# First attention: the value products of a batch in one visit, with sixteen probability buffers

## The reference

```
qkv = x @ Wqkv + bqkv                 # x: layer-normed rows of the batch
qkv_a = xa @ Wqkv_aux + bqkv_aux      # xa: the batch's 375 context rows
dots = einsum('bhqd,bhkd->bhqk', q, k) * scale       # 16 heads, 112 keys of the batch itself
dots_aux = einsum('bhqd,bhkd->bhqk', q, ka) * scale  # 375 keys of the context
h_main = softmax(dots) @ v
h_aux = softmax(dots_aux) @ va
out = h_main * (1 - sigmoid(g)) + h_aux * sigmoid(g)
return out @ Wo + bo
```

## Time and profile before

| what | value |
|---|---|
| median of three runs | 784.34 us (781.73 to 785.57) |
| span of the profiled execution | 792.0 us |
| PE busy | 724.7 us, 91% of the span, 6719 instructions |
| PE weight loads busy | 568.2 us, 6720 instructions |
| VectorE busy | 418.0 us, 53% |
| ScalarE busy | 326.5 us, 41% |
| a step of the first attention, from 301.50 | 23.38 us, PE busy 23.32 |

### The profile page before, as it was taken

How to read it: one execution, slowest core, us unless ns; L and a number is a source line. 1 busy time by engine, 2 the same in 40 slices (tenths; PEclk the granted TensorE clock), 3 DMA queues, 4 the chain that set the end, 5 groups by cost and what they waited for, 6 DMA issues and landing times. The chain is left out here.

```text
span 792.0 us, 19429 instructions
## 1 busy us (share of the span) xinstructions
PE 724.7 (91%) x6719; PEld 568.2 (72%) x6720; DVE 418.0 (53%) x1267; ACT 326.5 (41%) x884; POOL 219.5 (28%) x361
## 2 busy tenths in 40 slices
PE   4688999999999999998998699998999988999996
PEld 2445777666677766676665588888788778999995
DVE  2366777787777687774772322222488762111111
ACT  2215655566555566654544133331465551101110
POOL 2402332233332232330312013333355532111111
PEclk9869999999999999999999789999999998999999
DMA  4999977998888998885946549882566642999950
GB/s 154 130 137 118 165 113 120 126 123 134 145 140 146 150 144 118 147 141 81 121 129 191 141 120 246 247 220 63 170 197 205 195 131 60 306 337 335 334 174 16
DMA packets 98984, 128.12 MB, mean 162 GB/s; under 512 B 23363, under 2 KB 83884, under 8 KB 98769
## 3 DMA queue, kind: packets, MB, share of 16 engines
q1 hardware_dynamic: 90625, 115.24, 68.0%
q0 software_dynamic: 3824, 8.46, 4.1%
q10 hardware_dynamic: 4447, 3.30, 1.8%
HBM read 74.68 MB, written 23.88 MB: 124 GB/s over the span
## 5 line engine op out<-in xcount | busy, mean ns | idle before, releaser
L549 ACT ACTIVATE probs<-psum 128x448 f32<-128x448 f32 (+2 forms) x256 | 125.2, 541 | 60.5 <-PE psum L883 59.9
L755 DVE TENSOR_REDUCE neg_max<-psum 112x2 f32<-112x750 f32 x128 | 118.8, 928 | 8.9 <-PE psum L866 7.3
L866 PE MATMUL psum<-stacks 96*128 96x487 bf16 (+1 forms) x256 | 78.3, 389 | 8.6 <-DMA stacks<-q_parts 5.8
L883 PE MATMUL psum<-stacks 102*128 102x112 bf16 (+1 forms) x1024 | 77.5, 215 | 3.6 <-DMA stacks<-mt 2.0
L898 PEld LDWEIGHTS psum<-probs,rings 128*32 128x32 f32 (+2 forms) x2048 | 45.3, 109 | 46.9 <-issue 37.6
L883 PEld LDWEIGHTS psum<-stacks 102*128 102x128 bf16 (+1 forms) x1024 | 54.7, 99 | 33.0 <-ACT probs L549 23.9
L898 PE MATMUL psum<-probs,rings 128*32 128x112 f32 (+2 forms) x2048 | 76.7, 266 | 0.8 <-issue 0.8
L1947 PEld LDWEIGHTS psum<-e_xt,rings 128*128 128x128 f32 x512 | 59.5, 192 | 2.2 <-ACT e_xt L1893 1.3
L1947 PE MATMUL psum<-e_xt,rings 128*128 128x112 f32 x512 | 59.7, 275 | 0.9 <-ACT e_xt L1893 0.9
L1913 DVE SCALAR_TENSOR_TENSOR e_y<-psum,e_x_in 112x256 f32<-112x256 f32 x16 | 7.7, 484 | 98.0 <-PE psum L1961 98.0
L1961 PE MATMUL psum<-rings,e_hid 128*112 128x256 f32 x256 | 57.9, 379 | 1.3 <-DVE e_hid L1920 1.3
(11 more groups left out here) (226 smaller groups left out, 1389.2 us busy)
## 6 DMA issues: line engine op xcount, KB each, us to landing
rings<-in_L_ffn_w SPq DMA_DIRECT2D x32, 1024.0 KB, 7.1
stacks<-rings SPq DMA_DIRECT2D x96, 243.5 KB
ct_dram<-rings SPq DMA_DIRECT2D x16, 375.0 KB, 10.8
a_ct<-ct_dram SPq DMA_DIRECT2D x16, 375.0 KB, 5.1
a_ctx<-in_ctx SPq DMA_DIRECT2D x16, 375.0 KB
stacks<-q_parts SPq DMA_DIRECT2D x96, 56.0 KB
rings<-in_ctx SPq DMA_DIRECT2D x16, 256.0 KB
w<-in_L_ffn_W SPq DMA_DIRECT2D x8, 512.0 KB, 11.5
```

The costliest lines, as they stand in the source:

```text
L549: nc.scalar.activation(probs[k % 4][0:keys, :, :], src, ACT.Exp, scale=DH ** -0.5).then_inc(s["exp_done"], 1)
L755: nc.vector.tensor_reduce(neg_max[:, 0, h:h + 2], psum[0:T, pair:pair + 2, 0:S], AX, ALU.max, negate=True)
L866: last = nc.tensor.matmul(bank[2 - 2 * (k % 2) + j][0:rows, 0:KV], q_flat[n.third][0:QK, h * T:h * T + rows], k_stack[n.third][0:QK, h, :] ...
L883: last = nc.tensor.matmul(bank[4 + k % 2][0:wide, j * T:(j + 1) * T], k_flat[n.third][:, first:first + wide], q_stack[n.third][:, h, :], s ...
```

## The change

For batches 0 to 13 all sixteen calls of `values` stand in one visit behind the eight slots. For that the probabilities of a batch have sixteen buffers: five of their own, two in the space of tensors used earlier, nine in the space of the first weights of experts 4 to 7, which are therefore loaded in step 16, behind `pv_done` of batch 13, and no longer in steps 10 to 13. `exp` waits for a buffer only in the last two batches, which keep the interleaved order and four buffers.

Where the values stood in a slot, between logits and scores, there is now one product that makes value rows (`make_values`, f32, 256 columns, two PE instructions), now of batch `b-2`, into banks 6 and 7; the copies of these rows by ScalarE stand behind the tenth and the sixteenth `exp`. Batch 15 has its value products still in the tail of step 16.

In the tail the turns of `xn`, context and maxima come before the router's turn, and the first keys products before the router's logits. On VectorE the router's normalisation moves out of the slots to behind the split maxima, the layer norm goes ahead of the normalised outputs, and the router's choice behind the rest of the keys. ScalarE copies and sends `mt` ahead of the router's copy.

```diff
...
+        probs = [sb(f"probs{k}", [P, 4, T]) for k in range(5)]
+        probs += [early([P, 4, T]) for _ in range(2)]
+        late_w1 = g_.w1[:, EARLY_W1:E0, :, :].rearrange("p e k f -> p (e k f)")
+        probs += [late_w1[:, k * 4 * T:(k + 1) * 4 * T].rearrange("p (j q) -> p j q", j=4) for k in range(9)]
...
-                        act.wait_ge(s["pv_done"], n.count(16, max(k - 3, 0)))
+                        if n.c >= LAST_APART:
+                            act.wait_ge(s["pv_done"], n.count(16, max(k - 3, 0)))
...
+                if b.c == B:
+                    sp.wait_ge(s["pv_done"], 16 * LAST_APART)
+                    for e in range(EARLY_W1, E0):
+                        load_expert(Item(0, e, E0))
...
                     if (b - 4).real():
                         if k == 1:
                             r.stats(dve, b - 4, xs, s["x1_ready"])
-                        if k == 5:
-                            r.norm(dve, b - 4, xs)
...
+                if (b - 4).real():
+                    r.norm(dve, b - 4, xs)
+                if (b + 1).real():
+                    ln(b + 1)
                 if (b - 3).real():
                     normalise(b - 3, 0)
                     normalise(b - 3, 1)
-                if (b + 1).real():
-                    ln(b + 1)
-                if (b - 4).real():
-                    r.choose(dve, b - 4, r.bias[:, :])
...
                     rest_k(b, 1)
+                if (b - 4).real():
+                    r.choose(dve, b - 4, r.bias[:, :])
...
+            def make_values(n, k):
+                c, h = k // 2, k % 2
+                at = v_bank(n)
...
+                made = nc.tensor.matmul(to, left, right, start=(h == 0), stop=(h == 1))
...
                     if (b - 3).real():
                         logits(b - 3, 2 * pair)
                         logits(b - 3, 2 * pair + 1)
+                    if (b - 2).real() and b.c <= B:
+                        make_values(b - 2, pair)
                     if (b - 2).real():
                         max_scores(b - 2, pair)
-                    if (b - 3).real():
-                        if pair >= 1:
-                            values(b - 3, 2 * pair - 2)
-                            values(b - 3, 2 * pair - 1)
-                if (b - 3).real():
+                    if last_ones and pair >= 1:
+                        values(b - 3, 2 * pair - 2)
+                        values(b - 3, 2 * pair - 1)
+                if last_ones:
                     values(b - 3, 14)
+                elif (b - 3).real():
+                    for k in range(16):
+                        values(b - 3, k)
```

More of the change, by code:

```diff
@@ L578, in step @@
                     act.dma_start(q_stack[n.third][QK:ROWS, :, :], mt[:, :]).then_inc(s_mr[n.parity], 16)
[L579 to L589, removed]
+                if (b - 4).real():
+                    r.copy_in(act, b - 4)
+                if b.c == B + 3:
+                    setup_copies()
+                if b.c == B:
+                    values_of_first(b - 1)
+                    values_of_rest(b - 1)
                 if (b - 3).real():
@@ L890, in values @@
                 pe.wait_ge(s["exp_done"], n.count(16, k + 1))
-                if k in (0, 8) and (n - 1).real():
-                    pe.wait_ge(s["mixed_ready"], (n - 1).count(2, k // 8 + 1))
+                if k in (0, 8):
+                    if n.c < LAST_APART:
+                        pe.wait_ge(s["v_ready"], (n + 1).count(3, 1 + k // 4))
+                    else:
+                        pe.wait_ge(s["mixed_ready"], (n - 1).count(2, k // 8 + 1))
                 keys, chunk, o = (T, 3, 0) if c == 0 else (CHUNKS[c - 1][1], c - 1, 1)
@@ L898, in values @@
                     last = nc.tensor.matmul(bank[6 + g // 2][32 * j:32 * j + 32, col:col + T], v[n.parity][0:keys, chunk, h, :],
-                                            probs[k % 4][0:keys, j, :], start=(c <= 1), stop=(c == 0 or c == 3))
+                                            probs_of(n, k)[0:keys, j, :], start=(c <= 1), stop=(c == 0 or c == 3))
                 last.then_inc(s["pv_done"], 1)
+            def make_values(n, k):
+                c, h = k // 2, k % 2
+                at = v_bank(n)
+                if k in (0, 4) and n.c < B - 1 and (n - 2).real():
+                    pe.wait_ge(s["mixed_ready"], (n - 2).count(2, 1 + k // 4))
+                if c < 3:
+                    lo, keys = CHUNKS[c]
+                    to, left, right = bank[at + c // 2][0:keys, c % 2 * D:(c % 2 + 1) * D], ct[n.parity][:, h, lo:lo + keys], w_aux[:, h, D:2 * D]
+                else:
+                    to, left, right = bank[at + 1][0:T, D:2 * D], xt[n.parity][:, h, :], w_x[:, h, 2 * D:3 * D]
+                made = nc.tensor.matmul(to, left, right, start=(h == 0), stop=(h == 1))
+                if k == 3:
+                    made.then_inc(s["v01_mm"], 1)
+                if k == 7:
+                    made.then_inc(s["v23_mm"], 1)
             def total(n):
@@ L964, in step @@
                     pe.wait_ge(s_mr[n.parity], n.turn(16, 16))
+                last_ones = (b - 3).real() and (b - 3).c >= LAST_APART
                 for pair in range(8):
@@ L986, in step @@
                     turn_context(b, 1)
-                if (b - 4).real():
-                    if (b - 3).real():
-                        pe.wait_ge(s["exp_done"], (b - 3).count(16, 15))
-                    r.turn(pe, b - 4, ident)
-                if (b - 3).real():
-                    values(b - 3, 15)
-                if b.real():
                     pe.wait_ge(s["xn_ready"], b.count(1, 1))
@@ L1009, in step @@
                                         ident16[0:T, 0:T]).then_inc(s["mt_mm"], 1)
+                if (b - 4).real():
+                    if (b - 3).real():
+                        pe.wait_ge(s["exp_done"], (b - 3).count(16, 15))
+                    r.turn(pe, b - 4, ident)
+                if last_ones:
+                    values(b - 3, 15)
                 if (b - 3).real():
@@ L1043, in step @@
                 if b.real():
-                    pe.wait_ge(s["xt_ready"], b.count(1, 1))
-                    pe.wait_ge(s["ct_ready"], b.count(2, 2))
-                    if (b - 2).real():
-                        pe.wait_ge(s["mt_ready"], (b - 2).count(1, 1))
-                    if not b.looped() and b.c == 0:
-                        pe.wait_ge(s["w_made"], 6)
-                        pe.wait_ge(s["bias_ready"], 1)
-                    keys_of(b, 1)
                     for h in range(2):
```

81 lines of the change are left out of this document (47 added, 34 removed).

## The result

The changed kernel takes 827.82 us in the median of 4 runs (822.66 to 831.55), the kernel before 784.96 (781.73 to 787.0): ratio 1.053, 95% interval 1.0486 to 1.0574. The forecast was 804 with 774 to 824; the direction was right, the size was less than half (19 of 43 us), and the time lies outside the range. The profiled execution has a span of 827.3 us.

The account below looks back on a forecast made before the run. PE's instruction list was taken to bound the step. On the profiled execution 792.0 - 4 (steps) - 6.4 (old stalls) + 25.5 (late code) + 5 (clock) = 812.1 us; that execution is 7.7 above the median, so 804.4, range 774 to 824.

Parts of the forecast that it names:

- twelve candidate blocks: Of 31 code blocks from step 3 to 16, twelve are used up in 3.7 to 8.0 us and may come late.
- The visit: Value products on PE: one visit of 128 costs 3.18 us a step instead of 4.16, 0.98 less.
- the value rows: Their products leave PE's tail (3.46 us) and stand in the slots, eight times 0.43; sum nothing.
- the new wait: PE's count waits 1.0 to 1.1 us a step for the router's choice on VectorE, leaving a gain of 0.3.
- The late weights: 2 MB for experts 4 to 7 now come in step 16, at no cost.
- the code term: Code blocks come late on PE: eleven stalls, 25.5 us, plus 5 us of lower clock.
- the lower pair of the earlier trace: The shorter two of four block times before stalls in the kernel before; 7.8 us a block was taken from them.
- the upper pair: The longer two of those block times, 10.00 and 10.09 us, taken as not typical.
- The clock: PE's lower clock behind stalls above 2.6 us: six at 1.74 would be 10 us, half taken, 5.
- the drain: End of the attention: taken at nothing, within 1.5 us either way, with the router's normalisation later there.
- blocks in time: Rival: PE's code comes early enough that the visit costs no stall; 774 to 780 us, chance 0.21.
- The choice that doesn't hold the count: Rival: PE's count doesn't wait for the router's choice; each step gains 1.3 us, -17 in all, chance 0.05.

Follow-up runs that it names:

- e1: Changed kernel with the copies into the stacks cut to one head of sixteen from batch 3 on: 791.04 us, ratio to before 1.0023.
- e2: Changed kernel with 128 semaphore increments put on PE at the start of step 3, moving every block edge by 128 instructions: 855.18 us, ratio 1.0855.
- e9: Changed kernel with four stack copies under way instead of up to twelve and the router's choice ahead of the rest of the keys: 787.31 us, ratio 1.001.
- e6: Kernel of e1 with 4 to 32 semaphore increments as idle time on PE behind the visit in five steps: 805.80 us in its one run.
- e4: Changed kernel with the router's choice put back ahead of the rest of the keys on VectorE: 830.08 us, ratio to before 1.0521.
- e11: Kernel of e9 with three stack copies under way instead of four: 788.54 us, ratio to before 1.0046.
- e13: Kernel of e9 with the fill's copies not held back and the router's normalisation back in the slots from step 17 on: 787.06 us, ratio 0.9988.
- e10: Kernel of e9 with six stack copies under way instead of four: 813.74 us, ratio to before 1.0375.

## Why the prediction was wrong

**The mechanism was right.** Blocks of 256 instructions, stalls at their ends and twelve candidate blocks stood in the prediction. Ten stalls came, five in the value products and five behind them, and e1, e2 and e9 show the mechanism by taking the copies away, moving the edges and thinning the queue. The visit, the value rows and the new wait came out near their sums: a step free of stalls takes 22.94 against a forecast of 23.1, and the count waits 0.78 against 1.0 to 1.1. The late weights show no wait of their own; whether they lengthened the stall of step 16, a step with a DMA share of 1.04, was not tried.

**The step that failed is the size of the code term, in both halves.** The block's time was put at 7.8 us, the lower pair of the earlier trace rows; over the ten stalls it was 8.7. I had taken the upper pair for untypical because most blocks before were not late. But whether a block is late tells little of its time here. By the packets and by counting rows, the blocks of the changed kernel that are asked for 6.6 to 12.3 us into a step, late or not, had landed 5.9 to 8.7 us after their edge; those asked for in the first 5 us of a step, or from 14 us on, at most 5.8 after it. A block that a visit will use up is asked for where the queue is full. Stalls sum to 33.5 us instead of 25.5, 8 more. That lies inside the bounds that the prediction gave.

**The clock is the larger miss.** It was put at 5 us, half of six times 1.74. Steps 4 to 15 took 313.1 us: twelve times 22.94, 25.3 of stalls, and 12.6 beyond both, of which 11.3 stand in the six steps with a lower clock. Step 16 is longer than in e1 by 29.00 - 21.67 - 5.67 = 1.7 beside its stall, step 3 longer than in e2, where it has none, by 28.69 - 24.65 - 2.60 = 1.4: 14.4 us in all. All eight stalls of 2.0 us and more are followed by a lower clock in this profile, the two of 1.3 by none. The eight cost 0.8 to 3.2 us each, 1.8 in the mean. So the 1.74 of the single case in the earlier trace rows was a fair price; what failed is the half, which was taken without a reason, and the count, eight instead of six (at 7.8 us a block only five of the forecast's stalls exceed 2.6; the sixth equals it). e6 shows that idle time alone can bring such a cost.

The two together make 47.9 instead of 30.5, 17.4 of the 22.8 us by which step 18 began later than forecast (42.9 against 20.1). Beside them stand 3.7 in step 17 (the forecast put the drain at nothing, within 1.5), 0.9 in step 16 (21.67 in e1, 20.78 before), 0.9 in the fill and 1.2 in steps 4, 10 and 13; the steps gained 5.7 instead of 4. Step 17 can be split by its clock, here and in e4:

```profile
436.14:458.26 22.12, 20.33 (x252) 14.32 (x250) 15.05 (x42) 9.78 (x22) 2.43 (x4) 0.85 0.22 69
...
435.03:454.65 19.62, 17.51 (x251) 11.66 (x249) 14.81 (x42) 9.78 (x22) 2.43 (x4) 1.00 0.08 19
```

At full clock it takes 19.6 to 19.7 in e2, e4 and e11, 1.2 more than the 18.43 before; the other 2.5 came with a clock of 0.85. That is not the stall of step 16 by itself, since e4 has one of 5.8 there. What the 1.2 are stays open; e13 shows that it is not the place of the normalisation alone.

**The range** ended at 824, the upper end of the forecast, with a block at 9.0 us and 10 us of clock: its clock term was too low even there. **The rivals:** blocks in time is nearly what e1 shows (791, with other routing and two stalls left), and the forecast of 774 to 780 for it was too low. Its steps 4 to 15 did gain 10.3 us (276.7 against 287.0), but the fill, step 3 and steps 16 and 17 cost 8, so that step 18 starts at 413.36, 2 us sooner than before and not 10.4. The choice that doesn't hold the count is e4: 0.9 us in a step without a stall and 6.5 over steps 4 to 15, with stalls 5 us longer. The Trainium skill's "mostly hidden" ("Runtime: NRT & Kernel Launch", "Instruction fetch mechanics") held for the kernel before, for all but four blocks of these steps, and failed for this one, where ten blocks cost 33.5 us.

## What to carry to other kernels

Count instructions for each stretch, not only their time: where a block of 256 is used up faster than the next one comes at that load of the DMA queues (here 3.2 us against 8.7), the order that looks shorter can be slower. Short products are best mixed with long ones, or the copies held back so that few are under way; the depth has to be tried, since two were too few here, six too many, and four or three about even. No variant here was faster than the kernel before. And price a stall with the clock behind it: in the changed kernel a stall of 2 us and more cost 0.8 to 3.2 us beyond itself.

## What the runs showed of the hardware that was not expected

The fetch depends on how much is queued, not on how much is moved: with the same bytes in a step, four copies under way gave stalls up to 2.7 us, six up to 5.1, twelve up to 6.0, and a late block took 4.9 to 6.0 us with four (8.1 in one case) and 7.3 to 10.7 with twelve, at DMA shares of 1.00 and 1.03 in the two stretches shown of e9's step 16 and the changed kernel's step 12.

Idle time by increments of a semaphore lowers the granted clock as a late block does: behind gaps of 2.44 and 4.35 us in e6 PE was busy 1.5 us longer. The length of the gap does not settle it. Behind 1.49 (e6) and 2.98 (e10) nothing changed; behind 1.59 (e10) and 1.76 (late code in step 7 of e6, which took 26.24) PE was busy 1.7 and 1.6 us longer.

And an increment on PE's queue is not free: 18 more of them lengthened e6's gap from 1.49 to 4.35 us, 0.16 each, and 128 took 21.4 in e2.
